# A GRU scan fused with an expert layer: where the row addition's waits stand, how many idle products fill PE, and a second PSUM bank behind the scan

## The reference, cut to what matters

```python
def cell(h, x):                                  # 256 steps, 8 sequences, width 512
    gi, gh = x @ W_ih + b_ih, h @ W_hh + b_hh
    i_r, i_z, i_n = jnp.split(gi, 3, axis=-1); h_r, h_z, h_n = jnp.split(gh, 3, axis=-1)
    r, z = sigmoid(i_r + h_r), sigmoid(i_z + h_z)
    n = tanh(i_n + r * h_n)
    return (1.0 - z) * n + z * h
hs = scan(cell, cond_2048, x)                    # every h is a token: 2048 of them
# feed-forward over the tokens: 8 experts (512 -> 2*256 -> 512), the best two of each token,
# and one shared expert (512 -> 2*1024 -> 512)
routed = sum over the token's two experts of weight * (silu(g) * u) @ w_down[e]
shared = (silu(g) * u) @ w_sh_down
y = x + routed + shared
```

## Time and profile before

| | |
|---|---|
| device time, 3 runs | 1250.64 us median (1248.44 to 1251.01) |
| device time of the profiled execution | 1243.78 us |
| its span | 1241.9 us |
| PE, DVE, ACT, POOL busy | 1041.9, 861.0, 573.5, 206.1 us |
| mean granted TensorE clock | 0.989 |
| DMA, mean | 147 GB/s |

### The profile page before, as it was taken

The page is one execution under the profiler, slowest core; times in us unless marked ns, Lnnn a source line. Parts: engine busy times, 40 slices in busy tenths (PEclk is TensorE's granted clock), DMA queues, the critical chain, the costliest instruction groups (busy, mean ns, idle before and its releaser), DMA issues.

```text
span 1241.9 us, 35936 instructions
## 1 busy us (share of the span) xinstructions
PE 1041.9 (84%) x13472; PEld 625.9 (50%) x13472; DVE 861.0 (69%) x4089; ACT 573.5 (46%) x1877; POOL 206.1 (17%) x213
## 2 busy tenths in 40 slices
PE   2789887778998898899889989997998888788874
PEld 2556555455654455455545545554545444454542
DVE  5898888688888786777777767777777777611111
ACT  5755555555454443344435434443444443425442
POOL 0100100201011212111211121112111222223332
PEclk9899999999999999999999999999999999999998
DMA  8923554638164641722362326232514253569673
GB/s 304 418 75 100 206 209 161 126 123 304 36 246 153 197 145 20 262 87 44 36 213 78 53 27 220 72 61 71 202 29 146 36 152 123 181 219 281 194 234 55
DMA packets 66911, 183.15 MB, mean 147 GB/s; under 512 B 7738, under 2 KB 40289, under 8 KB 59169
## 3 DMA queue, kind: packets, MB, share of 16 engines
q1 hardware_dynamic: 45632, 107.74, 24.2%
q0 software_dynamic: 21104, 73.11, 22.9%
HBM read 137.01 MB, written 52.87 MB: 153 GB/s over the span
## 4 chain that ended last, share of the span: by engine, by line
PE 45%; DVE 26%; DMA 12%; issue 8%; ACT 8%; POOL 0%; POOLq 0%; SPq 0%; ACTq 0%; DVEq 0%
PE psG L702 15%; PE psG L708 14%; DMA y<-arena 8%; DVE arena L1031 5%; DVE arena L1029 5%; PE psU L765 4%; ACT arena L1413 3%; ACT arena L1409 3%; DVE arena L1053 3%; DVE arena L1039 3%; DVE arena L1041 3%; DVE arena L1049 3%; PE psG L838 3%; PE psD L777 2%; DVE arena L1033 2%
## 5 line engine op out<-in xcount | busy, mean ns | idle before, releaser
L702 PE MATMUL psG<-arena 128*32 128x384 f16 x4096 | 214.4, 330 | 95.8 <-DVE arena L1053 87.0
L1409 ACT ACTIVATE arena<-arena 128x32 f32<-128x32 f32 x256 | 58.5, 229 | 354.9 <-DVE arena L1033 347.0
L708 PE MATMUL psG<-arena 128*32 128x384 f16 x4096 | 215.1, 327 | 5.8 <-issue 5.7
L765 PE MATMUL psU<-arena 128*128 128x256 f16 (+1 forms) x1920 | 201.5, 252 | 0.9 <-issue 0.6
L1029 DVE STREAM_TRANSPOSE arena<-psG 128x128 f32<-128x128 f32 x256 | 81.0, 316 | 173.7 <-PE psG L708 168.6
L702 PEld LDWEIGHTS psG<-arena 128*32 128x32 f16 x4096 | 86.3, 96 | 194.6 <-DVE arena L1053 156.2
L765 PEld LDWEIGHTS psU<-arena 128*128 128x128 f16 x1920 | 157.1, 98 | 50.2 <-issue 14.2
L1598 POOL DMA_INDIRECT y<-arena x55 | 88.4, 1606 | 399.1 <-ACT arena L1506 172.7
L708 PEld LDWEIGHTS psG<-arena 128*32 128x32 f16 x4096 | 110.8, 97 | 65.1 <-issue 8.9
L809 PE MATMUL psS<-arena 128*128 128x512 f16 x468 | 116.5, 379 | 15.9 <-DVE arena L1253 10.6
L1031 DVE STREAM_TRANSPOSE arena<-psG 128x256 f32<-128x256 f32 x256 | 104.0, 406 | 0.0
(11 more groups left out here) (162 smaller groups left out, 1598.3 us busy)
## 6 DMA issues: line engine op xcount, KB each, us to landing
arena<-expert_weights SPq DMA_DIRECT2D x39, 1536.0 KB, 9.1
arena<-wgu POOLq DMA_DIRECT2D x32, 512.0 KB, 6.0
expert_weights<-arena POOLq DMA_DIRECT2D x9, 1536.0 KB, 5.6
gi_scratch<-arena SPq DMA_DIRECT2D x84, 128.0 KB, 3.1
arena<-gi_scratch SPq DMA_DIRECT2D x14, 768.0 KB, 7.3
arena<-wd POOLq DMA_DIRECT2D x16, 512.0 KB, 6.1
arena<-x SPq DMA_DIRECT2D x8, 512.0 KB, 3.7
hidden_rows<-arena SPq DMA_DIRECT2D x16, 256.0 KB
```

Of the source, the lines that this page charges most:

```text
L702: e.matmul(psG[32 * j:32 * j + 32, 0:384], prev[:, c, 2:6].rearrange("p q n -> p (q n)"), whv[c][1][:, :, :, 32 * j:32 * j + 32], start=(c ...
L708: r = e.matmul(psG[32 * j:32 * j + 32, 0:384], prev[:, c, 0:4].rearrange("p q n -> p (q n)"), whv[c][0][:, :, :, 32 * j:32 * j + 32], star ...
L765: r = e.matmul(psU[u % 2][:, 256 * gu:256 * gu + width], half(W_GS + ex * 4 + c, pw)[:, o:o + 128], hh[:, 1 - ph, c, first:first + width], ...
L1409: e.activation(Ur, Ur, ACT.Tanh, scale=reg_tr).then_inc(th_r, 1)
```

## The change

There are three edits. (1) `add_rows` now writes its wait on `added` first and the wait on its own data second, so the two change places: `added` stands on the transfer's instruction, `e_ev` or `s_ev` in an instruction ahead of it. (2) `warm` gets `int((1.45 - load) / 0.165)` products in place of `int((1.7 - load) / 0.165)`: eight for ten, and 205 for 258 in all. (3) Behind the scan, blocks 24, 26, up to 38 take the bank psG, which the scan used, for `up`, and the others keep psS. `up(k, 0)` then waits until DVE has read block k-2, not k-1.

```diff
+        def up_bank(k):
+            return psG if k > KS and (k - KS) % 2 else psS
...
-                    need(e, e_up, k)
+                    need(e, e_up, k if k < KS else k - 1)
...
+                    if k == KS + 1:
+                        e.wait_ge(tr_zn, T)
...
-                    r = e.matmul(psS[:, 0:512], hT[k % 2][:, ph, c], ew_half(k, c, pw),
+                    r = e.matmul(up_bank(k)[:, 0:512], hT[k % 2][:, ph, c], ew_half(k, c, pw),
...
-                    warm(t, int((1.7 - PLAN.load("PE", t)) / 0.165))
+                    warm(t, int((1.45 - PLAN.load("PE", t)) / 0.165))
...
-                e.scalar_tensor_tensor(out=x_, in0=x_, scalar=col(C_UP[1]), in1=psS[:, 256:512],
+                e.scalar_tensor_tensor(out=x_, in0=x_, scalar=col(C_UP[1]), in1=up_bank(k)[:, 256:512],
...
-                e.activation(Xe[k % 2], psS[:, 0:256], ACT.Silu, scale=reg_tg[1]).then_inc(e_gate, 1)
+                e.activation(Xe[k % 2], up_bank(k)[:, 0:256], ACT.Silu, scale=reg_tg[1]).then_inc(e_gate, 1)
...
-            def add_rows(index, out, no):
+            def add_rows(index, out, no, ready, v):
+                need(e, added, 16 * no)
+                e.wait_ge(ready, v)
                 if no == 0:
                     for k in range(2):
                         e.wait_ge(st_y[k], 16 * (NBLK // 2))
-                need(e, added, 16 * no)
                 e.indirect_dma_start(y, by(index), out, None, compute_op=ALU.add).then_inc(added, 16)
...
             def s_add(q):
-                e.wait_ge(s_ev, q + 1)
-                add_rows(tok_u[:, q:q + 1], so[q % 2], ADDS[("s_add", q)])
+                add_rows(tok_u[:, q:q + 1], so[q % 2], ADDS[("s_add", q)], s_ev, q + 1)
...
             def add(k):
-                e.wait_ge(e_ev, k + 1)
-                add_rows(rid[:, k:k + 1], ob[k % 2], ADDS[("add", k)])
+                add_rows(rid[:, k:k + 1], ob[k % 2], ADDS[("add", k)], e_ev, k + 1)
```

## The result

The changed kernel takes 1239.52 us (median of 4 runs, 1237.47 to 1241.29), the kernel before 1250.1 us on the same chip. The ratio is 0.9916, with a 95% interval of 0.9894 to 0.9938. The time on record was 1239.4 us. The profiled execution took 1238.16 us, and its span is 1236.3 us.

A forecast was written before the change was run, and what follows sets the result against it. The prediction took the tail's chain of additions to y, and the step's chain in the scan, as the bound. 8.3 + 2.9 = 11.2 us, taken from the median of 1250.64, gave 1239.4 us, range 1235.0 to 1245.5.

The forecast's parts named there:

- The waits of the addition: Tail, edit 1: 17 handovers between additions fall from 0.86 to 0.28 us each, 9.8 us gross, 8.3 us net.
- the swap gives nothing: Rival, 5%: an indirect transfer prepares itself only after a landing, 0.8 us stay per handover; 1247.7 us.
- The handover that held 1.67 us of issue: Tail: whether its extra 1.0 us goes with the wait was unknown; half, 0.5 us, was taken off the gain.
- The first addition of the chain: Start of the tail: released by its data last, it now pays the preparation, 0.5 us off the gain.
- At the end the additions catch up with the blocks: End of the tail: the last additions wait for their data again, 0.5 us off the gain.
- the transfers stretch: Rival, 25%: under load, sooner additions only queue longer; 5.5 of 9.8 us of handovers gain nothing; 1244.9 us.
- The idle products: Scan, edit 2: eight for ten idle products bring 18 steps from 3.97 to 3.81 us, 2.9 us gained.
- stalls move: Rival, 8%: PE's issue stalls in the scan fall elsewhere, a few us either way; result within 2.5 us of before.
- The second bank: Tail, edit 3: PE gains about 0.37 us a block, blocks come every 6.6 us, nothing gained by itself.
- without edit 3 about 1 us of edit 1 would be lost: Tail: blocks every 6.93 us would not keep ahead of additions every 6.6 us, costing about 1 us.
- The price of a low step: Scan, rival that the clock falls in lightened steps, 4%: 0.64 us more per low step; 1258.6 us if all 30 are low.
- Both signs of being wrong: Last addition starting later than about 1226 us plus the scan's change; scan's end not moving by 2 to 4 us.

The follow-up runs named there:

- before_copy: The kernel before, unchanged, profiled on the slower chip of the experiments: 1247.3 us in one run.
- e4_small_loads: The changed kernel, but the tail's ten loads of weights fetch a quarter of their columns, on a faster chip: 1200.17 us in one run.
- e13_swap_banks: Edits 1 and 3 against the kernel before, ten idle products kept, on the slower chip: 1240.18 us, ratio 0.9938.
- after_again: All three edits once more, against the kernel before on the slower chip: 1234.64 us, ratio 0.9878.

## Why the prediction came out right, step by step

**The waits of the addition (8.3 us).** The mechanism was right. Each handover is 0.27 us (0.39 in some, 0.43 in one), not 0.75 to 0.97, for an indirect transfer released by a landing too, so the rival that the swap gives nothing is out. The gross gain is 9.3 us against 9.8. The handover that held 1.67 us of issue is gone too (it stands in before_copy as well, and in no kernel with edit 1), so the half of it that was taken off was not needed. The first addition of the chain starts at 1119.41, 0.79 us behind its data, where it was 0.28, as foreseen. At the end the additions catch up with the blocks: the last but one starts at 1224.75, 0.76 us behind its own `out_` and 0.43 us behind the landing, which costs some 0.2 us and not 0.5.

The size was off by what the transfers took back, 2.9 us in the first trace (104.9 - 102.0). The net of the distance is 6.4 us, and of the whole of edit 1 5.8 us with the first addition's 0.5 taken off. Alone it measured 6.5 and 5.5 us. So the term of 8.3 us was too large by about 2 to 3 us, and the rival *the transfers stretch* holds in part. Its price was set too high (5.5 us of handovers lost). That loads in flight make the additions long is shown by e4_small_loads (21 us). That sooner issues alone make them longer, as the rival has it, is not: with edit 1 alone the transfers took what they took before. There the missing part is in the handovers, where additions waited for their blocks.

**The idle products (2.9 us).** The rule of 3.97 to 3.81 us held in 18 steps, as forecast, except where one stalled, with a sum of 2.6 to 3.1 us. On two chips a stall at step 92 took 2.2 to 2.7 us of it, and on the slower one steps 45 and 46 grew by 1.1 and 1.3 us from e13_swap_banks to after_again. In the first two traces the rule gave its 2.9 us, and the scan is only 0.1 us shorter. Between the traces of kernels with and without edit 2, 0.1 to 2.3 us are left in the scan. This is the rival *stalls move*, which had 8% by itself. It came on top of the forecast and not in its place.

**The second bank (nothing by itself).** PE's wait on DVE's reading is gone, as forecast, and blocks come every 6.5 us (forecast 6.6). One sentence of the prediction fell: that without edit 3 about 1 us of edit 1 would be lost. Without it the handovers are 2 to 3 us longer and the transfers 1 to 3 us shorter. The distance is the same within what traces of one kernel differ by (109.5 to 111.0).

**The clock.** Eight products hold it, at 0.986 to 0.994 on average in the profiled executions with them, against 0.988 to 0.994 with ten and 0.966 with none. The price of a low step was set at half of what it is. The trace doesn't bear out the rule on groups that go through banks by turns ("TensorE: Matmul & The Clock Gate" of the Trainium skill, "A second HAM failure mode: psum-queue depth-cycling"): in the tail the blocks do take two banks by turns, and the granted clock of the window from 1119 to 1162 us is 1.00. It falls once later, to 0.58 in the window from 1197 us, behind PE's wait of 2.57 us for a gather and not between such groups.

**The sum.** The total agrees (1239.4 and 1239.52 us), and that it does so to 0.1 us is luck. Both signs of being wrong that the prediction gives did come: the last addition starts at 1229.66 and not by 1226, and the scan's end moved by 0.3 us and not by 2 to 4. The sum of 11.2 us stands beside 10.6 us measured here, 14.0 on the slower chip of the experiments and 6.4 on a faster one. Of the profiled executions' own difference, 5.6 us in the first pair, 6.4 us are the distance's; the scan gave only 0.3, and the first addition's later start took 1.1. That execution of the kernel before was the fastest of its runs, 6.3 us under their median. Since the sum was made against it and then shifted to the median, that did not spoil the forecast. But about 5 of the 10.6 us between the medians are in no trace of this pair.

What stays open: the stalls' cause, why they cost some 27 us more on one chip, and why there the medians moved by 5 us more than the traces.

## What to carry to other kernels

- If an indirect transfer has two waits, the one that comes last should stand on the instruction itself, and the earlier one ahead of it. This is worth 0.5 us each time, if the earlier one comes at least 0.5 us before the last. Other instructions were not tried. Look for it wherever the chain shows a sequencer row and then half a us of issue.
- In a chain of transfers the price of the gap is only half of it. With the DMA engines over 0.9 busy, the transfers' own length moves too: with all three edits 1.1 of 8.5 us and 2.9 of 9.3 us of the handovers' gain came back as longer transfers. One run with smaller loads shows what the limit behind it is.
- Idle products that hold the clock need only reach the moment at which the real ones can start. Eight of them did it here as well as ten, and none cost 1.26 us in each step that went low. The gain can be lost elsewhere, since the stalls of the scan move with the instruction stream.

## What the runs showed of the hardware

- The preparation of an indirect transfer (about 0.5 us) lies ahead of a wait that the instruction carries, and behind one in a separate instruction: 0.27 and 0.79 us from landing to start.
- An addition of 128 rows of 512 takes mostly 4.6 to 5.1 us with small loads (two of 17 took 6.0, e4_small_loads), and the ten beside loads of 1.5 MB that the prediction counts take 5.4 to 8.9 us (the changed kernel).
- The same program takes 31 us more on one chip than on two others, some 27 us of it in long single steps of the scan. In the stalls that were looked at, PE or DVE waits for nothing that the profile names. Which steps stall depends on the instruction stream: two idle products fewer brought a stall of 2.2 us at a step that had none.
